# Moving the one-column shift of the relative-position bands from the read to the write, with buffers on 256-byte lines

## The reference

```
scores = jnp.einsum('bhqd,bhkd->bhqk', q, k)
dist_idx = pos_l - pos_r + M - 1
pos_emb = dist_emb[dist_idx]
rel_q = jnp.einsum('bhld,lrd->bhlr', q, pos_emb)
rel_k = jnp.einsum('bhrd,lrd->bhlr', k, pos_emb)
scores = (scores + rel_q + rel_k) / jnp.sqrt(D)
probs = jax.nn.softmax(scores, axis=-1)
```

## Time and profile before

| | us |
|---|---|
| median of 3 runs | 4512.68 |
| lowest and highest | 4507.69 and 4517.39 |
| the profiled execution | 4511.1 |
| its span from first to last instruction | 4509.4 |

### The profile page before, as it was taken

The page is one execution under the profiler, slowest core; times in us unless marked ns, Lnnn a source line. Parts: engine busy times, 40 slices in busy tenths (PEclk is TensorE's granted clock), DMA queues, the critical chain, the costliest instruction groups (busy, mean ns, idle before and its releaser), DMA issues. The chain is left out here.

```text
span 4509.4 us, 68206 instructions
## 1 busy us (share of the span) xinstructions
PE 3803.1 (84%) x19584; PEld 2402.4 (53%) x19584; DVE 2256.6 (50%) x6132; ACT 1741.0 (39%) x3691; POOL 1861.8 (41%) x1684
## 2 busy tenths in 40 slices
PE   6888888888888876689999999999798676778686
PEld 4666666666666652256666666666443441112144
DVE  4767776677666766834444444444333211111155
ACT  4666666666666652333333333333211000000023
POOL 3666776667766763334444444444311000000012
PEclk9999999999999998899999999999899787889798
DMA  6999999999999984554544544445355328999713
GB/s 258 396 378 379 373 389 376 390 375 375 389 385 380 378 343 152 171 187 147 168 159 157 168 148 165 163 153 169 118 170 161 108 73 341 411 409 409 306 64 130
DMA packets 566768, 1169.16 MB, mean 259 GB/s; under 512 B 35312, under 2 KB 225136, under 8 KB 517360
## 3 DMA queue, kind: packets, MB, share of 16 engines
q1 hardware_dynamic: 561968, 1158.57, 69.8%
q10 hardware_dynamic: 4032, 7.34, 0.4%
q0 software_dynamic: 512, 0.26, 0.0%
HBM read 762.63 MB, written 403.44 MB: 259 GB/s over the span
## 5 line engine op out<-in xcount | busy, mean ns | idle before, releaser
L433 POOL TENSOR_SCALAR a_sc<-a_sc,a_inv 128x512 f32<-128x512 f32 x512 | 818.4, 1602 | 385.5 <-DVE a_inv L383 323.4
L996 POOL TENSOR_SCALAR b_sc<-b_sc,b_inv 128x128 f32<-128x128 f32 (+3 forms) x512 | 552.7, 1082 | 777.7 <-DVE b_inv L949 777.7
L908 ACT ACTIVATE b_sc<-b_sc,b_mx 128x128 f32<-128x128 f32 (+3 forms) x512 | 287.7, 562 | 815.3 <-DVE b_mx L943 815.2
L284 ACT ACTIVATE a_stage_q<-a_ps_q 128x640 f32<-128x640 f32 x512 | 359.9, 703 | 467.1 <-PE a_ps_q L201 437.7
L954 DVE COPY b_pt<-b_ps_t 128x128 f32<-128x128 f32 (+3 forms) x512 | 248.5, 485 | 575.6 <-PE b_ps_t L856 575.6
L390 DVE COPY a_pt<-a_ps_t 128x512 f32<-128x512 f32 x512 | 353.6, 691 | 276.1 <-PE a_ps_t L187 238.2
L376 DVE CUSTOM_DVE_ANT_0 a_sc<-a_ps_s,a_rq 128x512 f32<-128x512 f32 x512 | 353.9, 691 | 201.9 <-PE a_ps_s L177 155.7
L274 ACT ACTIVATE a_sc<-a_sc,a_mx 128x512 f32<-128x512 f32 x512 | 370.4, 723 | 80.4 <-DVE a_mx L376 79.0
L175 PE MATMUL a_ps_s<-a_ks,a_qs 128*128 128x512 f32 x512 | 262.1, 512 | 140.5 <-DMA a_rk<-band_k 104.6
L284 ACT ACTIVATE a_stage_k<-a_ps_k 128x640 f32<-128x640 f32 x512 | 359.0, 701 | 32.1 <-DMA band_k<-a_stage_k 32.1
L187 PEld LDWEIGHTS a_ps_t<-a_ident,a_sc 128*128 128x128 f32 x2048 | 250.5, 145 | 217.2 <-issue 202.2
(11 more groups left out here) (201 smaller groups left out, 6486.4 us busy)
## 6 DMA issues: line engine op xcount, KB each, us to landing
band_q<-a_stage_q SPq DMA_DIRECT2D x128, 1280.0 KB, 9.3
band_k<-a_stage_k SPq DMA_DIRECT2D x128, 1280.0 KB, 11.9
a_rk<-band_k SPq DMA_DIRECT2D x128, 1024.0 KB, 13.9
a_rq<-band_q SPq DMA_DIRECT2D x256, 512.0 KB, 14.6
d_w<-in_e_W SPq DMA_DIRECT2D x32, 4096.0 KB, 38.8
b_xT<-x1T SPq DMA_DIRECT2D x64, 1024.0 KB, 5.7
b_cT<-in_ctxT SPq DMA_DIRECT2D x64, 1024.0 KB, 8.3
d_wg<-in_e_Wg SPq DMA_DIRECT2D x16, 4096.0 KB, 28.9
```

Of the source, the lines that this page charges most:

```text
L284: act.activation(st[h % 2][:, t, :].rearrange("p (a n) -> p a n", a=2), src[:, :, 0:WIN // 2], ACT.Copy).then_inc(sem[f"a_{kind}_staged"], 1)
L433: pool.tensor_scalar(sc[n][:, :], sc[n][:, :], inv[:, n:n + 1], None, ALU.mult)\
L908: act.activation(sc[i][:, 0:width(i)], sc[i][:, 0:width(i)], ACT.Exp, bias=mx[:, i:i + 1], scale=-1.0, accum_out=sm[:, i:i + 1]).then_inc( ...
L996: pool.tensor_scalar(sc[i][:, 0:width(i)], sc[i][:, 0:width(i)], inv[:, i:i + 1], None, ALU.mult).then_inc(sem["b_normed"], 1)
```

## The change

Three things are changed in `self_attention` and its scratch tensors.

- The write to DRAM now shears: `skewed` puts row p at element 1 + p x 2561 of the slot (row pitch 2560 plus one). The read is straight: `straight` takes partition p at element 128 + p x 2560. The same elements arrive at the same places. The four tiles of a partition are still written as one run of 10,240 bytes, and a read row is still 2048 bytes.
- A slot is longer by 3 x 64 floats (`BAND`), for the shift at its start and its end. Each slot begins on a 256-byte line, and so does each row of each read; a written row begins 4 bytes further into a line with each partition.
- A filler `a_line` of 128 bytes comes first on chip, and the small buffers are moved behind the large ones. All large buffers of this stage then begin on 256-byte lines on chip.

```diff
+LINE = 64
+ROW = T4 * WIN
+BAND = P * ROW + 3 * LINE
...
+        sb("a_line", [P, 32])
         xT = sb("a_xT", [P, K4, S])
         wq, wk, wv = (sb(f"a_w{n}", [P, K4, E]) for n in "qkv")
-        cols = sb("a_cols", [P, H // HQ, 3])
...
-        emask = sb("a_emask", [P, 2])
...
-        mx, sm, inv = (sb(f"a_{n}", [P, SC]) for n in ("mx", "sm", "inv"))
...
+        cols = sb("a_cols", [P, H // HQ, 3])
+        emask = sb("a_emask", [P, 2])
+        mx, sm, inv = (sb(f"a_{n}", [P, SC]) for n in ("mx", "sm", "inv"))
...
-                    out = dr[f"a_band_{kind}"][j % 2, h]
-                    sp.dma_start(out, st[h % 2][:, :, :]).then_inc(sem[f"a_{kind}_written{h % 2}"], 16)
-
-            def sheared(kind, j, t0, nt):
-                b = dr[f"a_band_{kind}"]
-                base = (j % 2 * HQ + t0 // T4) * P * T4 * WIN + t0 % T4 * WIN + P - 1
-                return bass.AP(tensor=b.tensor, offset=base, ap=[[T4 * WIN - 1, P], [WIN, nt], [1, S]])
+                    sp.dma_start(skewed(kind, j, h), st[h % 2][:, :, :].rearrange("p t n -> p (t n)")).then_inc(sem[f"a_{kind}_written{h % 2}"], 16)
+
+            def skewed(kind, j, h):
+
+                return bass.AP(tensor=dr[f"a_band_{kind}"].tensor, offset=(j % 2 * HQ + h) * BAND + 2 * LINE - (P - 1),
+                               ap=[[ROW + 1, P], [1, ROW]])
+
+            def straight(kind, j, t0, nt):
+                return bass.AP(tensor=dr[f"a_band_{kind}"].tensor,
+                               offset=(j % 2 * HQ + t0 // T4) * BAND + 2 * LINE + t0 % T4 * WIN,
+                               ap=[[ROW, P], [WIN, nt], [1, S]])
...
-                sp.dma_start(rk[h][:, :, :], sheared("k", j, T4 * h, T4)).then_inc(sem[f"a_rk{h}"], 16)
+                sp.dma_start(rk[h][:, :, :], straight("k", j, T4 * h, T4)).then_inc(sem[f"a_rk{h}"], 16)
...
-                    sp.dma_start(rq[n][:, :, :], sheared("q", j, T4 * h + 2 * half, 2)).then_inc(sem[f"a_rq{n}"], 16)
+                    sp.dma_start(rq[n][:, :, :], straight("q", j, T4 * h + 2 * half, 2)).then_inc(sem[f"a_rq{n}"], 16)
```

More of the change, by code:

```diff
@@ L1788, in attention_views @@
         "xT": batch(t["xT"], QUADS // B), "a_cols": t["a_cols"],
-        "a_band_q": scratch("band_q", (2, HQ, P, T4, WIN)),
-        "a_band_k": scratch("band_k", (2, HQ, P, T4, WIN)), "a_ctxT": lambda q: ctx1[q],
+        "a_band_q": scratch("band_q", (2 * HQ * BAND,)),
+        "a_band_k": scratch("band_k", (2 * HQ * BAND,)), "a_ctxT": lambda q: ctx1[q],
         "na_wo": chunks(t["attn_Wo"]), "na_bo": bc(t["attn_bo"]), "gamma": bc(t["attn_ln_gamma"]),
```

## The result

The changed kernel takes 4521.95 us (median; 4513.24 to 4529.18), the kernel before 4510.06 us (4499.16 to 4519.61). The ratio is **1.0028, with a 95% interval of 1.0021 to 1.0035**: some 12 us slower. That is inside the predicted range (4470 to 4575), but outside the likeliest case, which was no change within 0.2%.

The account below looks back on a forecast made before the run. The prediction took the DMA engines in self-attention to bound the kernel. Terms of 0 for issue, engines, reads, writes and on-chip side left 4511.1 us, with the median 1.6 higher at 4513; range 4470 to 4575 us.

Parts of the forecast that it names:

- the likeliest case: Whole kernel: no change within 0.2% (9.0 us), a time of 4513 us; chance 0.38.
- The bound: Self-attention: DMA engines have no time left, queue shares add up to 99.1% from 200 to 1600 us.
- The price per ns: Self-attention DMA: 1 ns on each read row is 8.2 us of the kernel, on each written row 2.0 us.
- excess: Self-attention DMA time above 84.5 ns per read and 387 ns per write; 86 us for the stage before the change.
- Issue and engines, 0: SP's transfer issue and compute engines' on-chip addresses: cost 0, SP having 821.9 us of waiting as cover.
- Reads on lines, 0: Self-attention DRAM reads: starting on 256-byte lines gains 0, as straight reads (84.8 ns) match sheared ones (84.5 ns).
- Writes off lines, 0: Self-attention DRAM writes: starting off lines costs 0, bounded between 0 and 297 us.
- The slower rival: Self-attention writes: lines torn between neighbouring rows cost 14.5 ns per written row, 30 us, giving 4543 us; chance 0.32.
- its marks: Profile after: best writes over 391 ns, or slow windows (532) over more of a write pair, and longer band_q, band_k landings.
- The on-chip side, 0: Self-attention buffers moved onto 256-byte lines on chip: gain taken as 0, bounded by 86 us.
- The sum: Whole kernel: 4511.1 us plus five terms of 0; the median of runs stands 1.6 above, 4513 us.
- the floors stay: Self-attention DMA: best prices remain 387 ns per written row and 84.5 ns per read row.

Follow-up runs that it names:

- the alternating order: SP issues write q, read k, write k, read q, on the version with whole-line writes, sheared reads and moved buffers: 4491.53 us, 0.9961 of the kernel before.

## Why the prediction was right or wrong

**The bound** was right: the DMA engines of this stage set the time, and the rest of the program together moved by only 1.7 us. The price per ns (8.2 us for a read row, 2.0 for a written one) is its upper end: of the 26 us of added excess 12 showed, as there was some idle DMA time to fill first. (Of the first 15 slices, the first moves 258 GB/s and not 340 to 400; nothing rests on it.)

**Issue and engines, 0**: right. The gain of the moved buffers is in the DMA's packets.

**Reads on lines, 0**: right, and for the stated reason. Straight and sheared reads differ by about 0.1% in both pairs of runs, once in either direction. The Trainium skill's page "DMA: Bandwidth & Descriptors", section "How a descriptor splits into AXI transactions", would by the prediction's estimate have had the reads give back 44 us; on the DRAM side the runs don't show it.

**Writes off lines, 0**: this is the step that failed. It was taken "by the only pair of rows that compares a start on a line with one off it", which was a pair of reads. Measured, with the chip's side equal, it is 23 us (0.9977 to 1.0028), 27 us (0.9967 to 1.0028) or 32 us (0.9957 to 1.0028), that is 11 to 16 ns for each written row. The slower rival had the mechanism, a torn line that the neighbour shares, and put 14.5 ns and 30 us on it. The size was right, though it was a guess, a tenth of a way between two rows. Of its marks one failed (writes at their best stay at 387 ns, not over 391) and two came: 13.3% against 7.2% of the written rows take over 450 ns, and the landings grew against the earlier trace rows, as the page's DMA issues of after show:

```profile
band_q<-a_stage_q SPq DMA_DIRECT2D x128, 1280.0 KB, 10.0
band_k<-a_stage_k SPq DMA_DIRECT2D x128, 1280.0 KB, 12.7
```

It had the piece too large: 64 bytes off is free, 4 bytes off is not. That the memory fetches a piece to complete it was only argued, and stays so. What the runs show is that rows further apart lose most of the price, and that the slow rows stand next to reads.

**The on-chip side, 0**: wrong as well. It was read from prices at the floor, where 224 and 128 bytes past a line look alike. Much of the gain sits in packets a few ns above the floor, and no row had a buffer on a line. It is 10 us alone and 32 us beside the torn writes.

**The sum.** Two terms of 0 that were +23 and -10 gave 4513 against 4521.95; the error of 9 us is small because they have opposite signs. That the time came so near is luck. "No change" was the likeliest case at 0.38, and the outcome is the one at 0.32. The forecast that the floors stay (387 and 84.5) held, and the price of the slow stretch hardly moved (532 to 537); the mistake was to look there for the change.

## What to carry to other kernels

- When a shift or a shear must be made by one side of a round trip through DRAM, make it in the read. In this kernel written rows that begin on multiples of 64 bytes cost nothing, and rows one word off cost 23 to 32 us. If they must be off, put them a line apart, which took the changed kernel from 1.0028 to 0.9982.
- In a stage bound by DMA, put small buffers behind the large ones and start the large ones on 256-byte lines on chip. It costs 128 bytes, and was worth 0.23% here alone, none of which shows in the median packet.
- A cost read from packets at their best says nothing about the share of time that is spent away from it. And a pair of rows on reads doesn't price a write.

The best version of this study keeps the sheared read, writes on lines and moves the buffers: 0.9967 (0.9956 to 0.9979) of before, 4493.79 us, and 0.9961 with the alternating order, which can't be told from it.

## What the hardware did that I hadn't expected

- On chip, buffers 128 bytes past a 256-byte line gave no gain (1.0004), on the line 0.9967. Of the sheared reads 70%, 82% and 95 to 96% took the floor of 84 ns with the buffers 224, 128 and 0 bytes past a line.
- Written rows of 10 KB that begin 4 bytes off cost 0.5 to 0.7% of the kernel, those 64 bytes off nothing, with no change in the best price of a row (387 ns) in either. No offset between 4 and 64 bytes was run.
- The two alignments interact: torn writes cost 44 us with buffers off lines and 23 us with buffers on them. Only with both off did most written rows take longer than 387 ns (68% of them).
